# An embedding tower on one NeuronCore: two more tables read by one-hot products, fewer and paced gathers, another order of layers

## What is computed

```python
e = jnp.stack([tbl_0[ids[:, 0]], ..., tbl_26[ids[:, 26]]], axis=1)   # 512 x 27 x 128
dot = jnp.einsum('bnd,bmd->bnm', e, e)
z = dot.reshape(512, 27 * 27)[:, pairs_i_below_j]                     # 351 numbers
h = jnp.concatenate([z, dense_ctx], axis=1)                           # 367
h = jnp.maximum(h @ W_top1 + b_top1, 0.0)                             # 512
h = jnp.maximum(h @ W_top2 + b_top2, 0.0)                             # 256
y = h @ W_top3                                                        # 1
```

## Time and profile before

| | us |
|---|---|
| median of three runs | 122.61 |
| lowest and highest | 122.23, 122.92 |
| the profiled execution | 122.14 |
| its span in the trace | 120.3 |

### The profile page before, as it was taken

How to read it: one execution, slowest core, us unless ns; L and a number is a source line. 1 busy time by engine, 2 the same in 40 slices (tenths; PEclk the granted TensorE clock), 3 DMA queues, 4 the chain that set the end, 5 groups by cost and what they waited for, 6 DMA issues and landing times.

```text
span 120.3 us, 2184 instructions
## 1 busy us (share of the span) xinstructions
PE 110.2 (92%) x733; PEld 97.7 (81%) x733; DVE 81.5 (68%) x253; ACT 76.9 (64%) x208; POOL 70.3 (58%) x73
## 2 busy tenths in 40 slices
PE   6699999997799999899699994999989999999992
PEld 6288878884677888688499894999979999999991
DVE  6999899959983999693078797126792348872121
ACT  4479996989909899883378785235773348881310
POOL 7777777777777877777777767777770000000000
PEclk9999999999999999999999999999999999999999
DMA  2999977757277379811212222122220000000000
GB/s 65 254 237 193 207 180 205 193 132 204 64 196 178 80 196 361 273 50 44 68 44 52 57 69 67 46 56 53 62 76 25 0 0 13 15 0 15 5 5 1
DMA packets 5662, 12.16 MB, mean 101 GB/s; under 512 B 2252, under 2 KB 2988, under 8 KB 5523
## 3 DMA queue, kind: packets, MB, share of 16 engines
q1 hardware_dynamic: 3580, 7.80, 24.3%
q0 software_dynamic: 2048, 4.20, 14.2%
q10 hardware_dynamic: 22, 0.02, 0.1%
HBM read 11.77 MB, written 0.00 MB: 98 GB/s over the span
## 4 chain that ended last, share of the span: by engine, by line
PE 42%; POOL 28%; DMA 11%; issue 8%; DVE 5%; SPq 4%; ACT 1%; POOLq 0%
POOL emb L353 26%; PE gram_ps L420 14%; PE acc L435 9%; DMA emb<-in_tbl,ids_sb 5%; DMA pairs<-pairs 5%; PE acc L455 5%; DVE pairs L513 4%; SPq L322 4%; PE tr_ps L367 3%; PE gram_ps L435 3%; PE acc L392 3%; PE acc L398 3%; PE tr_ps L455 1%; POOL embT L342 1%; ACT embT L600 1%
## 5 line engine op out<-in xcount | busy, mean ns | idle before, releaser
L353 POOL DMA_INDIRECT emb<-in_tbl,ids_sb x64 | 68.1, 1064 | 19.3 <-issue 19.2
L513 DVE COPY pairs<-gram_ps 26x56 f32<-26x56 f32 (+1 forms) x128 | 26.0, 203 | 11.2 <-PE gram_ps L420 9.5
L553 DVE TENSOR_SCALAR onehot<-idrel 125x512 fp32r<-125x512 f32 x81 | 29.3, 430 | 5.3 <-ACT idrel L614 5.2
L420 PE MATMUL gram_ps<-embT 128*122 128x104 f32 x256 | 30.1, 272 | 1.5 <-ACT embT L600 1.1
L420 PEld LDWEIGHTS gram_ps<-embT 128*122 128x122 f32 x256 | 28.5, 187 | 2.9 <-ACT embT L600 1.5
L513 ACT COPY pairs<-gram_ps 26x56 f32<-26x56 f32 (+1 forms) x128 | 24.9, 194 | 7.7 <-PE gram_ps L420 6.1
L392 PE MATMUL acc<-onehot,hi 125*128 125x512 f32 x92 | 25.0, 417 | 1.0 <-ACT hi L622 1.0
L398 PE MATMUL acc<-onehot,lo 125*128 125x512 f32 x92 | 22.8, 390 | 0.0
L392 PEld LDWEIGHTS acc<-onehot,hi 125*128 125x128 f32 x92 | 17.7, 199 | 5.1 <-ACT hi L622 1.7
L398 PEld LDWEIGHTS acc<-onehot,lo 125*128 125x128 f32 x92 | 17.2, 188 | 3.8 <-DVE lo L557 0.2
L600 ACT COPY embT<-acc 128x512 f32<-128x512 f32 x11 | 12.0, 1093 | 8.8 <-PE acc L398 8.8
(11 more groups left out here) (43 smaller groups left out, 59.6 us busy)
## 6 DMA issues: line engine op xcount, KB each, us to landing
table<-in_tbl SPq DMA_DIRECT2D x8, 480.0 KB
table<-in_tbl SPq DMA_DIRECT2D x2, 600.0 KB
emb<-in_tbl,ids_sb POOLq DMA_INDIRECT x64, 3.3
w_sb<-in_W SPq DMA_DIRECT2D x1, 1024.0 KB, 6.6
w_sb<-in_W SPq DMA_DIRECT2D x1, 512.0 KB, 8.5
table<-in_tbl SPq DMA_DIRECT2D x2, 240.0 KB
pairs<-pairs SPq DMA_DIRECT2D x16, 15.0 KB
table<-in_tbl SPq DMA_DIRECT2D x8, 20.0 KB
```

The source lines that it names most:

```text
L353: pool.indirect_dma_start(emb[:, t % EMB_RING, gathered_features.index(f), :], None, tables[f], bass.IndirectOffsetOnAxis(ids_sb[:, t, f:f ...
L420: last = nc.tensor.matmul(gram_ps[0:ROWS, u % 2, g, 0:WIDTH], vectors[:, QUAD * p0:QUAD * p0 + ROWS], embT[:, t, p0:p0 + SG, 1:FEATS], sta ...
L513: last = copy(pairs[QUAD * q:QUAD * q + FEATS - 1, t % 2, a:SLOTS, c0:c0 + UNITG], src.rearrange("r g a -> r a g"))
L553: nc.vector.tensor_scalar(one_hot(k, c), idrel[0:ROWS_K, b, 0:batch], float(c), None, ALU.is_equal).then_inc(onehot_by_dve, 1)
```

## The change

Tables 9 and 10 (1,250 rows, ten chunks each) pass from the gathered to the looked-up ones: 13 look-ups, 14 gathered features in groups of 4, 4, 4 and 2, 56 gathers. Groups move to other look-ups in AT_LOOKUP, and the first group of tile 2 joins them. The gathers of the first ten groups each wait for a number of one-hots of VectorE, those of later groups for the landing of the group before. The ids of the first look-up come by a DMA of their own, repeated on all 128 partitions, and VectorE makes `idrel` of look-up 0 from them; the other ids become floats on ScalarE. `pick` is one column per look-up, broadcast when read. `near` stands between the two halves of `hi` in look-ups 0 and 1. The zeroing moves behind the last look-up on VectorE. The last copy of looked-up vectors is split: tile 0, then the rest. The warm-up has three matmuls for five. In STEPS, h1(t - 1) stands behind all four units of tile t, h2 behind the next group's transposes, the last group's transposes directly ahead of the next tile's first unit, and y behind that unit.

```diff
-LOOKED_UP_TABLES = [4, 6, 3, 7, 8, 5, 11, 12, 15, 20, 21]
+LOOKED_UP_TABLES = [4, 6, 3, 7, 8, 5, 11, 12, 9, 15, 20, 10, 21]
...
+    PACED_GROUPS = 9
-    WARM = 5
+    WARM = 3
...
-        pick = sb("pick", [P, NK, P], F32R)
+        pick = sb("pick", [P, NK], F32R)
...
-        AT_LOOKUP = {2: ORDER[0], 3: ORDER[1], 4: ORDER[2], 5: ORDER[3], 6: ORDER[4], 8: ORDER[5], 9: ORDER[6], 10: ORDER[7]}
+        AT_LOOKUP = {2: ORDER[0], 4: ORDER[1], 5: ORDER[2], 6: ORDER[3], 8: ORDER[4], 9: ORDER[5], 10: ORDER[6], 11: ORDER[7], 12: ORDER[8]}
...
-        STEPS = tr(0, range(NFG)) + tr(1, range(NFG)) + [("gram", 0, n) for n in range(UNITS)]
+        STEPS = [("gram", 0, n) for n in range(UNITS)]
         for t in range(1, TILES - 1):
-            STEPS += [("gram", t, 0), ("gram", t, 1)] + tr(t + 1, [0]) + [("gram", t, 2), ("h1", t - 1, None)]
-            STEPS += tr(t + 1, [1]) + [("h2", t - 1, None)]
-
-            STEPS += [("gram half 0", t, 3)] + tr(t + 1, [2]) + [("y", t - 1, None)]
-            STEPS += tr(t + 1, [3]) + [("gram half 1", t, 3)]
+            STEPS += [("gram", t, 0)] + [("y", t - 2, None)] * (t >= 2) + [("gram", t, 1)] + tr(t + 1, [0])
+            STEPS += [("gram", t, 2)] + tr(t + 1, [1]) + [("gram", t, 3), ("h1", t - 1, None)]
+            STEPS += tr(t + 1, [2]) + [("h2", t - 1, None)] + tr(t + 1, [3])
         t = TILES - 1
-        STEPS += [("gram", t, u) for u in range(UNITS)]
+        STEPS += [("gram", t, 0), ("y", t - 2, None)] + [("gram", t, u) for u in range(1, UNITS)]
...
-            nc.gpsimd.memset(embT[:, 0:TILES // 2, :, FEATS:QUAD], 0.0).then_inc(pads_zeroed, 1)
...
+                    if tr_index(t, g) > PACED_GROUPS:
+
+                        preceding = ORDER[tr_index(t, g) - 1]
+                        pool.wait_ge(gathered[preceding[1]], rows_gathered(*preceding))
                     for f in group(t, g):
+                        n = t * len(gathered_features) + gathered_features.index(f)
+                        if n >= 4 and tr_index(t, g) <= PACED_GROUPS:
+
+                            pool.wait_ge(onehot_by_dve, 27 * n // 10 - 4)
...
+                if t == 1 and n == 0:
+
+                    pe.wait_ge(vectors_out, NK + 1)
...
-            spread_ids(0)
             spread_ids(1)
...
-            nc.vector.tensor_copy(id_rows_r[0:NK, :], id_rows[0:NK]).then_inc(id_rows_ready, 1)
-
-            nc.vector.memset(pairs[:, :, 0, :], 0.0)
-            nc.vector.memset(pairs[:, :, SLOTS - 1, :], 0.0).then_inc(pairs_zeroed, 1)
-            nc.vector.memset(embT[:, TILES // 2:, :, FEATS:QUAD], 0.0).then_inc(pads_zeroed, 1)
+            nc.vector.tensor_scalar(idrel[0:ROWS_K, 0, 0:batch], id_first[0:ROWS_K, :], base_f[0:ROWS_K, own(0)], None,
+                                    ALU.add).then_inc(first_idrel_ready, 1)
...
+            nc.vector.memset(pairs[:, :, 0, :], 0.0)
+            nc.vector.memset(pairs[:, :, SLOTS - 1, :], 0.0).then_inc(pairs_zeroed, 1)
+            nc.vector.memset(embT[:, :, :, FEATS:QUAD], 0.0).then_inc(pads_zeroed, 1)
...
-                nc.scalar.copy(embT[:, :, :, LOOKED_UP[k]],
-                               acc[:, k % 2, 0:batch].rearrange("d (t p) -> d t p", p=P)).then_inc(vectors_out, 1)
+                src = acc[:, k % 2, 0:batch].rearrange("d (t p) -> d t p", p=P)
+                for tiles in ([slice(0, TILES)] if k < NK - 1 else [slice(0, 1), slice(1, TILES)]):
+                    nc.scalar.copy(embT[:, tiles, :, LOOKED_UP[k]], src[:, tiles, :]).then_inc(vectors_out, 1)
...
+            act.dma_start(id_first[:, :], ids_looked_up[0].partition_broadcast(P)).then_inc(id_first_loaded, 16)
             act.dma_start(id_rows[0:NK], ids_looked_up).then_inc(id_rows_loaded, 16)
...
+            nc.scalar.copy(id_rows_r[0:NK, :], id_rows[0:NK]).then_inc(id_rows_ready, 1)
```

More of the change, by code:

```diff
@@ L163, in build_tower @@
         near = sb("near", [P, batch])
-        id_rows = near[:, :].bitcast(I32)
+        id_rows = sb("id_rows", [P, batch], I32)
+        id_first = sb("id_first", [P, batch], I32)
         tr_ps = pb("tr_ps", [P, 2, 4, P])
@@ L179, in build_tower @@
         base_f_ready = sem("base_f_ready")
+        id_first_loaded = sem("id_first_loaded")
+        first_idrel_ready = sem("first_idrel_ready")
         idrel_ready = sem("idrel_ready")
@@ L370, in spread_ids @@
             def spread_ids(k):
-                if k >= 2:
-                    pe.wait_ge(idrel_ready, k - 1)
-                nc.tensor.matmul(spread_ps(k), pick[:, k, :], id_rows_r[:, :],
+                if k >= 3:
+                    pe.wait_ge(idrel_ready, k - 2)
+                nc.tensor.matmul(spread_ps(k), pick[:, k:k + 1].broadcast_to([P, P]), id_rows_r[:, :],
                                  start=True, stop=True).then_inc(ids_spread, 1)
@@ L400, in look_up, with gram @@
                 last.then_inc(looked_up, 1)
-            def gram(t, n, groups):
+            def gram(t, n):
                 if t == 0 and n == 0:
                     pe.wait_ge(vectors_out, NK)
-                    pe.wait_ge(pads_zeroed, 2)
+                    pe.wait_ge(pads_zeroed, 1)
+                if t == 1 and n == 0:
+                    pe.wait_ge(vectors_out, NK + 1)
                 if n == 0:
@@ L417, in gram @@
                 vectors = embT[:, t, :, :].rearrange("d p f -> d (p f)")
-                for g in groups:
+                for g in range(UNITG):
                     p0 = SG * (UNITG * n + g)
@@ L421, in gram @@
                                             embT[:, t, p0:p0 + SG, 1:FEATS], start=True, stop=True)
-                if g == UNITG - 1:
-                    last.then_inc(gram_done, 1)
+                last.then_inc(gram_done, 1)
             def h1(t, slots):
@@ L490, in _ @@
                 elif kind == "gram":
-                    gram(t, arg, range(UNITG))
-                elif kind == "gram half 0":
-                    gram(t, arg, range(UNITG // 2))
-                elif kind == "gram half 1":
-                    gram(t, arg, range(UNITG // 2, UNITG))
+                    gram(t, arg)
                 elif kind == "h1 unmoved slot":
@@ L565, in _ @@
                     transposes(t, arg)
-                elif kind in ("gram", "gram half 1"):
+                elif kind == "gram":
                     if t >= 2 and arg == 0:
@@ L606, in _ @@
             nc.scalar.activation(warm[:, :], chunk[:, 0:1], ACT.Square)
+            act.wait_ge(id_rows_loaded, 16)
+            act.wait_ge(id_rows_zeroed, 1)
+            nc.scalar.copy(id_rows_r[0:NK, :], id_rows[0:NK]).then_inc(id_rows_ready, 1)
             act.wait_ge(base_f_ready, 1)
@@ L609, in _ @@
                 r, b = k % RING, k % 2
-                act.wait_ge(ids_spread, k + 1)
                 if k >= 2:
                     act.wait_ge(looked_up, k - 1)
-                nc.scalar.activation(idrel[0:ROWS_K, b, 0:batch], spread_ps(k)[0:ROWS_K, :],
-                                     ACT.Identity, bias=base_f[0:ROWS_K, own(k)]).then_inc(idrel_ready, 1)
+                if k >= 1:
+                    act.wait_ge(ids_spread, k)
+                    nc.scalar.activation(idrel[0:ROWS_K, b, 0:batch], spread_ps(k)[0:ROWS_K, :],
+                                         ACT.Identity, bias=base_f[0:ROWS_K, own(k)]).then_inc(idrel_ready, 1)
                 for n, c in enumerate(parts(k)):
@@ L622, in _ @@
                     nc.scalar.copy(hi[0:ROWS_K, b, c, :], table[0:ROWS_K, r, c, :]).then_inc(hi_ready, 1)
-                act.wait_ge(idrel_ready, k + 1)
-                nc.scalar.activation(near[0:ROWS_K, 0:batch], idrel[0:ROWS_K, b, 0:batch], ACT.Square,
-                                     bias=chunk[0:ROWS_K, own(k)]).then_inc(near_ready, 1)
+                    if n == 0:
+                        if k == 0:
+                            act.wait_ge(first_idrel_ready, 1)
+                        else:
+                            act.wait_ge(idrel_ready, k)
+                        nc.scalar.activation(near[0:ROWS_K, 0:batch], idrel[0:ROWS_K, b, 0:batch], ACT.Square,
+                                             bias=chunk[0:ROWS_K, own(k)]).then_inc(near_ready, 1)
                 act.wait_ge(near_ready, k + 1)
```

11 lines of the change are left out of this document (7 added, 4 removed).

## The result

| us | before | changed |
|---|---|---|
| median | 122.77 (4 runs) | 129.51 (4 runs) |
| lowest and highest | 122.23, 123.94 | 129.11, 130.07 |
| the profiled execution | 122.14 | 129.11 |
| its span in the trace | 120.3 | 127.3 |

The ratio is 1.054, with an interval of 1.045 to 1.063: slower, by 6.7 us by the medians and 7.0 by the profiled executions, where +5.0 was forecast. 129.51 is at the upper end of the range of 125.7 to 129.5. Some executions of a kernel take over 1.5% more than its fastest; medians hold all of them, ratios leave them out, and so a ratio can differ from that of two medians. On another chip the unchanged pair gave 129.0 against 122.47, a ratio of 1.070 (1.060 to 1.081).

What follows compares the result with a forecast made beforehand. TensorE, busy 110.2 of 120.3 us and working in order, was taken as the bound. Start -0.3, look-ups +7.7, into the units -0.35, units and layers -2.1 gave +5.0: 127.5 us, range 125.7 to 129.5 (126.4 to 128.6 at 60%).

Steps and rivals of the forecast that it cites:

- start, to the first transposes: Up to the first look-up: VectorE making `idrel` removes most of the 0.98 us wait for `hi`; -0.3 us, bounds -1.0 to +1.5.
- look-ups: First transposes to last copy: two more ten-chunk look-ups and spreads for eight transposes, waits for gathers gone; 42.73 to 50.4, +7.7 us.
- into the units: Last look-up to first unit: only a quarter copy is awaited, but the zeroing ends later; -0.35 us, bounds -0.6 and +0.5.
- units and layers: First unit onward: eight transposes -0.9, h1's waits -2.5, uncovered copies of the last transposes +1.3; sum -2.1 us.
- behind the last unit: From the last unit on nothing is moved, and tile 3's moved rows come as before: 0 us.
- 0.5 left over: In the look-up stretch, 0.5 us of before's 42.73 that the counted parts and waits left over, added again to the forecast.
- Rival (d): Not slower: look-up matmuls draw closer without gathers running against them, 0.229 to 0.207 us or less, time 122.5 or below; 4%.
- Both waits of h1 on moved rows: In the layers: h1 stands one full unit (1.87 us) later, enough to remove waits of 1.7 and 0.8; -2.5 us.
- the uncovered copy: Before the first units of tiles 2 and 3: the last transposes' copy has no cover, 0.65 us twice, +1.3 us.
- the place 0.7 us after the last matmul: End of the look-ups: VectorE's memsets (`pads_zeroed`) end 0.7 us after the last matmul, against 0.45 for the copy.
- Rival (a): The start pays: repeated ids delay table 1, TensorE stays longer at 1.2 GHz; +1.1 and up to +0.8, 128.7 to 129.8; 15%.
- by it the start was to come at +0.8: Alternative for the start: with DMA engines shared between queues, the repeated ids delay the tables; +0.8 us instead of -0.3.

Runs made afterwards that it cites:

- Experiment 8: Changed kernel with the last group's transposes ahead of h2 and not behind it: 128.08 us against 129.0 for the changed kernel on the same chip.
- Experiments 1 and 3: 1: changed kernel without the repeated ids (start of before), 130.56 and 128.02 us on two chips; 3: changed kernel, extra DMA reading 128 different rows, 131.09 us.
- experiment 4: Kernel before with the DMA of the repeated ids added, its result unused: 170.79 us, where before took 157.54 on that chip.
- experiment 10: Changed kernel with 11 look-ups, no pacing, before's start, five warm-up matmuls, early memsets, last transposes ahead of h2: 121.65 us, ratio to before 1.011.

## Why the prediction was right in sign and short in size

By its own steps, in the profiled executions:

| step | forecast | measured |
|---|---|---|
| start, to the first transposes | -0.3 | +2.06 |
| look-ups | +7.7 | +6.97 (49.70 for 42.73) |
| into the units | -0.35 | +0.32 (1.39 for 1.07) |
| units and layers | -2.1 | -2.43 (44.62 for 47.05) |
| behind the last unit | 0 | +0.08 |
| sum | +5.0 | +7.0 |

**Look-ups.** The counting held: eight matmuls take 1.81 to 1.84, as in the earlier trace rows, and ten 2.27 to 2.46; no transposes wait for gathers; and the stretch is 0.7 shorter than summed, since nearly nothing of the 0.5 left over came back. Rival (d) is gone: the spacing is 0.227 to 0.229. The Trainium skill's figure of 131 ns ("TensorE: Matmul & The Clock Gate", "Back-to-back issue gap") is in no run here either.

**Units and layers.** Both waits of h1 on moved rows are gone, and the uncovered copy costs 90.33 - 89.44 - 0.22 = 0.67 each time, 0.65 forecast. Experiment 8 takes exactly that away.

**Into the units.** The mechanism was right (the memset ends last, not the copy), but the place 0.7 us after the last matmul was too early by 0.7. I had added up three durations; of the 0.7, the trace puts 0.48 down to idle time between the second memset and the third, as the earlier trace rows had already shown with 0.22 before the same instruction.

**The start** is the term that failed, by 2.4 us: forecast -0.3, measured +2.06. Rival (a), with its 15%, has the size: it said +1.1 and up to +0.8, and measured were +1.29 to the first look-up matmul and +0.8 in its sixteen matmuls. It also has half of the way. My step took the wait for `hi` as caused by ScalarE's `idrel`, and priced the extra DMA by its bytes at the rate of the earlier trace rows, 1.1 us at most. By the trace's landing records the first half of the first table comes at 6.45 us and came at 4.42 before, so it is 2.0 late, and `hi`, which had found it landed at 5.21, now begins at 6.53, behind a wait for it. What neither step nor rival told is that the ids are as late. The cast of `id_rows` stands ahead of `hi` on ScalarE, and its load stands behind `id_first` in the same queue; it landed 4.56 us after its issue, and the cast ends at 6.38. I had listed this cast among the things that ScalarE does first, and priced only its duration. By these figures either lateness alone would have held the first `hi` until about 6.4.

Experiments 1 and 3 show that the repeated ids are behind both: without their DMA the first look-up is 1.9 earlier, and of that 1.2 goes when the DMA reads different rows. The ids and the table move together in all of them, so no run parts the two. The gain that the step counted on is there beneath: with the same DMA and the old order of casts the first look-up is at 8.73 (experiment 4), and at 7.31 with the changed order on the same chip, 1.4 earlier. The Trainium skill's rule that queues of several engines share the DMA engines ("DMA: Bandwidth & Descriptors", "Issuing engines are not separate DMA queues") was the better guide: by it the start was to come at +0.8. The trace agrees: on SyncE's queue `ids_sb` lands after 4.1 us, and after 2.0 without the DMA on ScalarE's.

The 0.8 us of slower matmuls is not the change's alone. The first eight took 3.42 in before's profiled execution and 3.66 to 3.86 in every other trace of this study, those of kernels based on before among them; the next eight took 1.98 in it and 1.99 to 2.99 in the others, and 2.99 and 2.04 in two traces of the same kernel, on two chips. So the moment at which TensorE goes from 0.43 us for 512 columns to 0.23 (1.2 to 2.4 GHz) varies by about 1 us between traces, and before's profiled execution had it early. How much of the 0.8 is the change's own stays open: the medians, which hold other executions, differ by 6.7 us.

## What to carry to other kernels

Where an engine works in order and is 92% busy, count the instructions moved to it first: here that gave the sign and most of the size. Then follow each id, index or constant that the first instructions need back to its DMA, and ask what stands ahead of it in its own queue: a load that is broadcast from one row to 128 partitions is not a small load, and one placed first makes all others late. Ask the same of the first table: in this case it was as late as the ids. A zeroing costs nothing only where the trace shows its engine free until the time when the result is wanted, idle gaps around it included.

## What the hardware showed unexpectedly

**Reading one row many times.** 256 KB from one row of 2 KB landed after 4.6 to 5.1 us, from 128 different rows of another tensor after 3.6 (one trace), and a load of 54 KB issued at the same time on another queue after 4.1 to 4.3 and 3.2, against 1.9 to 2.1 without it.

**A chip on which other engines stand still while gathers are issued.** On one chip before took 154.4 to 159.3 us, and with one DMA more 164.9 to 176.3, while three forms of the changed kernel took 130.1 to 133.5, 0.84 of before's time in one of them (0.838 to 0.849). In the profile shown under experiment 4, VectorE and ScalarE stand still up to 33 us without a releaser while GpSimd issues gather upon gather. All three fast forms had the pacing, and both slow ones had not; but they also had 13 look-ups for 11 and 56 gathers for 64, and no unpaced form of the changed kernel ran on that chip. Whether the pacing is the cure, and whether the gathers take anything from the other engines, stays open. On the two other chips the unpaced kernels show nothing like it (129.45 without and 129.0 with pacing). If such chips are common, the changed kernel may be the better one though it loses 5 to 7% here.

**Steadiness.** On one and the same chip before ran between 119.77 and 125.17 in eleven runs, and the kernel of experiment 10, also unpaced, between 120.97 and 121.89 in six. I did not find out why.
